# Self-attention in halves of a tile: four heads' scores in a row, in the banks that then hold the other half's transposed probabilities

## The reference, cut to what matters

```
x = cross_attention(x, ctx)                      # (2, 2048, 512), 16 heads, bias, output projection
for layer in range(2):
    h = shift_token(x)                           # the second half of the channels comes from the token before
    q, k, v = split(h @ wqkv, 3)                 # 8 heads of 64
    q = l2norm(q) * q_scale;  k = l2norm(k) * k_scale
    q, k = rotary_xpos(q, k)                     # q*cos*scale + rotate_half(q)*sin*scale, k with 1/scale
    # windows of 256 tokens; a query sees its own window and the one in front, i-256 <= j <= i
    attn = softmax(where(mask, -inf, 8 * q @ k.T))
    x = x + (attn @ v) @ wo
    h = layernorm(shift_token(x)) * lg + lb
    a, g = split(h @ w1 + b1, 2)
    x = x + (a * gelu(g)) @ w2 + b2
```

## Time and profile before

| | us |
|---|---|
| time, median of 3 runs | 3585.88 (3585.81 to 3586.5) |
| the profiled execution | 3587.36 |
| its span | 3585.6 |
| PE busy in the span | 3447.5 (96%) |
| DVE busy | 2271.9 (63%) |
| ACT busy | 1500.6 (42%) |
| POOL busy | 1138.8 (32%) |
| one tile of attention, from transpose to transpose | 22.81 |

### The profile page before, as it was taken

How to read it: one execution, slowest core, us unless ns; L and a number is a source line. 1 busy time by engine, 2 the same in 40 slices (tenths; PEclk the granted TensorE clock), 3 DMA queues, 4 the chain that set the end, 5 groups by cost and what they waited for, 6 DMA issues and landing times. The chain is left out here.

```text
span 3585.6 us, 56360 instructions
## 1 busy us (share of the span) xinstructions
PE 3447.5 (96%) x20560; PEld 2795.2 (78%) x20560; DVE 2271.9 (63%) x4996; ACT 1500.6 (42%) x3978; POOL 1138.8 (32%) x1008
## 2 busy tenths in 40 slices
PE   7999996999999989999999989999999899999999
PEld 5676675888888877888888868888888678888887
DVE  6888875999999984222322259999999642333322
ACT  5666663555555543111111145555555421111111
POOL 3434433555555520000000045555555121101111
PEclk9999998999999999999999989999999999999999
DMA  4112213111121122111111121112111331111111
GB/s 123 42 45 64 71 42 124 57 55 58 61 68 60 57 73 88 44 44 43 42 43 44 64 75 57 57 55 75 57 59 53 97 111 40 46 49 49 40 41 38
DMA packets 186869, 216.26 MB, mean 60 GB/s; under 512 B 27094, under 2 KB 125654, under 8 KB 186595
## 3 DMA queue, kind: packets, MB, share of 16 engines
q1 hardware_dynamic: 186595, 212.65, 18.5%
HBM read 125.79 MB, written 69.00 MB: 54 GB/s over the span
## 5 line engine op out<-in xcount | busy, mean ns | idle before, releaser
L1893 DVE SCALAR_TENSOR_TENSOR u_full<-banks,b_cols,gate 128x512 f32<-128x512 f32 (+1 forms) x176 | 132.1, 751 | 875.4 <-ACT gate L1851 802.4
L46 PE MATMUL banks<-fxT_h,w_h 128*128 128x512 f32 (+1 forms) x1408 | 556.3, 395 | 3.0 <-DVE w_l L1877 2.6
L48 PE MATMUL banks<-fxT_h,w_l 128*128 128x512 f32 (+1 forms) x1408 | 556.1, 395 | 0.0
L47 PE MATMUL banks<-fxT_l,w_h 128*128 128x512 f32 (+1 forms) x1408 | 555.2, 394 | 0.0
L1851 ACT ACTIVATE gate<-banks,b_cols 128x512 f32<-128x512 f32 (+1 forms) x176 | 121.2, 689 | 1007.1 <-PE banks L48 1007.1
L1746 POOL TENSOR_TENSOR sums<-sums,b_rows 128x512 f32<-128x512 f32 x64 | 85.2, 1363 | 877.6 <-DMA sums<-z_rows 877.6
L1146 POOL TENSOR_TENSOR rn<-ssq,neg_half 128x8 f32<-128x8 f32 x128 | 210.8, 1647 | 412.3 <-DVE ssq L1419 405.9
L46 PE MATMUL banks<-wqkv_h,hT_h 128*128 128x512 f32 x768 | 324.9, 423 | 15.0 <-DVE wqkv_l L1406 15.0
L1355 ACT ACTIVATE pT_h<-banks 128x384 fp32r<-128x384 f32 (+2 forms) x512 | 213.9, 470 | 257.5 <-PE banks L1244 256.5
L1460 DVE TENSOR_SCALAR prob<-prob,rc 128x384 f32<-128x384 f32 (+2 forms) x512 | 313.5, 654 | 9.1
L46 PEld LDWEIGHTS banks<-fxT_h,w_h 128*128 128x128 f32 (+1 forms) x1408 | 259.6, 184 | 72.0 <-DVE w_l L1877 4.3
(11 more groups left out here) (190 smaller groups left out, 8183.2 us busy)
## 6 DMA issues: line engine op xcount, KB each, us to landing
y_rows<-sums SPq DMA_DIRECT2D x16, 1024.0 KB
sums<-y_rows SPq DMA_DIRECT2D x64, 256.0 KB, 3.0
z_rows<-sums SPq DMA_DIRECT2D x64, 256.0 KB, 2.0
sums<-z_rows SPq DMA_DIRECT2D x16, 1024.0 KB, 5.8
thirds<-in_w SPq DMA_DIRECT2D x30, 512.0 KB, 4.8
thirds<-in_x SPq DMA_DIRECT2D x8, 1024.0 KB, 6.8
x_rows<-thirds SPq DMA_DIRECT2D x8, 1024.0 KB, 4.3
thirds<-y_rows SPq DMA_DIRECT2D x64, 128.0 KB, 2.8
```

Source lines behind the costliest of these rows:

```text
L46: pe.matmul(out, a_h, b_h, start=start, stop=False)
L47: pe.matmul(out, a_h, b_l, start=False, stop=False)
L48: return pe.matmul(out, a_l, b_h, start=False, stop=stop)
L1893: e.scalar_tensor_tensor(out=u_full[r, m % 2, :], in0=ps[r, 2 * (m % 2), :], scalar=b1[r, place[m], 0:1], in1=gate[r, :], op0=ALU.add, op1 ...
```

## The change

The loop over t has two halves of four heads in place of four rounds of two. PE makes the scores of a whole half in a row: 12 matmuls into four banks, 2 to 5 (`bank_head`). The transposed probabilities of the half in front go into the same four banks, each as soon as the scores that lay there have been masked. `transpose_p` waits for that, and `scores` waits until the transposed probabilities in the banks have been split. In the first half of tile t stand the scores of its heads 4 to 7, v of t + 1, the transpose of t + 2, four transposed heads 0 to 3, q and k of t + 1, the projection of q of t + 2, and the values of heads 0 to 3. In the second stand the scores of heads 0 to 3 of t + 1, the projection of k of t + 2, the transposed heads 4 to 7, the output of t - 1, and the values of heads 4 to 7. `oT` has two buffers. The residual of t - 2 in place of t - 1 is added in tile t. POOL takes root, cosine and sine of q, then those of k. SP issues both copies of keys to the front slots at the same place in its list. The turns in banks 0, 1 and 7 are numbered anew with waits to match.

```
         def bank_qkv(t, a):
-            return turn(7 * t if a == 2 else 7 * t - 2 + a)
+            if (t, a) == (0, 2):
+                return O_BANK
+            return turn(7 * t if a == 2 else 7 * t - 3 + a)
...
+        def bank_head(h):
+            return S_BANK + h % LANES
...
-                    root(0)
-                    times_cos(0)
-                    root(1)
-                    plus_sin(0)
-                    times_cos(1)
-                    plus_sin(1)
+                    for a in range(2):
+                        root(a)
+                        times_cos(a)
+                        plus_sin(a)
...
-                def scores(t, p):
+                def scores(t, half):
...
+                    n = HEADS * t + LANES * half
...
-                    e.wait_ge(s["dv_s"], nth(LH, HEADS * t + 2 * p))
-                    for a, b in ((0, 0), (0, 1), (1, 0)):
-                        for odd in range(2):
...
+                    e.wait_ge(s["dv_s"], nth(LH, n))
+                    e.wait_ge(s["dv_t"], nth(LH, n - LANES))
+                    for p in range(2 * half, 2 * half + 2):
+                        for a, b in ((0, 0), (0, 1), (1, 0)):
+                            for odd in range(2):
...
                 def transpose_p(t, h):
                     n = HEADS * t + h
                     e.wait_ge(s["dv_p"], nth(LH, n + 1))
-                    e.wait_ge(s["dv_t"], nth(LH, n - 1))
+
+                    e.wait_ge(s["dv_s"], nth(LH, min(n + LANES + 1, LH)))
...
+                    if t:
+                        scores(t, 1)
+                    project(t + 1, 2)
+                    transpose_h(t + 2)
+                    if t == 0:
+                        scores(t, 1)
+                    for h in range(LANES):
+                        transpose_p(t, h)
+                    transpose_qk(t + 1)
+                    project(t + 2, 0)
+                    for h in range(LANES):
+                        values(t, h)
+
+                    scores(t + 1, 0)
+                    project(t + 2, 1)
+                    for h in range(LANES, HEADS):
+                        transpose_p(t, h)
+                    output(t - 1)
+                    for h in range(LANES, HEADS):
+                        values(t, h)
...
+                    lo_o(t - 1, 1)
+                    for h in range(LANES, HEADS):
+                        masked(t, h)
+                    residual(t - 2)
+                    lo_v(t + 1)
+                    lo_h(t + 2)
+                    for h in range(LANES):
+                        lo_p(t, h)
+                    lo_qk(t + 1)
+                    divide(t, 2)
+                    norms(t + 2, 0)
+                    divide(t, 3)
...
+                    lo_o(t, 0)
+                    normalise(t + 2, 0)
+                    for h in range(LANES):
+                        masked(t + 1, h)
+                    norms(t + 2, 1)
+                    for h in range(LANES, HEADS):
+                        lo_p(t, h)
+                    normalise(t + 2, 1)
+                    divide(t + 1, 0)
+                    divide(t + 1, 1)
```

More of the change, by code:

```diff
@@ L1099, in body @@
                                 load_piece(e, ahead["s"], w_next, n)
[L1100 to L1104, removed]
+                        if u == 2 and i < NI - 1:
+                            for slot in range(2):
+                                e.wait_ge(s["dv_r"], at(2 * NT, i, 8, 2 * (slot + 2) + 2))
+                                e.wait_ge(s["pe_s"], at(LH, i, 4 * HEADS, HEADS * (slot + 1)))
+                                for part in range(2):
+                                    e.dma_start(kT[part][:, :, slot, :].bitcast(F32), kT[part][:, :, slot + 4, :].bitcast(F32)).then_inc(s["k_copy"], 16)
                         store(i, u - 1)
@@ L1196, in project @@
                     e.wait_ge(s["dv_h"], nth(NT, t + 1))
[L1198 to L1201, removed]
+                    if a == 1:
+                        e.wait_ge(s["dv_r"], nth(2 * NT, 2 * t - 1))
+                    elif a == 2 and t:
+                        e.wait_ge(s["dv_norm"], nth(2 * NT, 2 * t + 1))
                     for k in range(DC):
@@ L1283, in _ @@
                 for t in range(NT):
-                    for p in range(4):
-                        if p < 3:
-                            scores(t, p + 1)
-                        else:
-                            scores(t + 1, 0)
-                        transpose_p(t, 2 * p)
-                        transpose_p(t, 2 * p + 1)
-                        if p == 0:
-                            project(t + 1, 2)
-                        elif p == 1:
-                            transpose_h(t + 2)
-                            output(t - 1)
-                        elif p == 2:
-                            transpose_qk(t + 1)
-                            project(t + 2, 0)
-                        else:
-                            project(t + 2, 1)
-                        values(t, 2 * p)
-                        values(t, 2 * p + 1)
+                    if t:
[17 more added lines that the diff above has]
+                        values(t, h)
                 output(NT - 1)
@@ new lines, in _ @@
+                    lo_o(t - 1, 1)
[4 more added lines that the diff above has]
+                    lo_h(t + 2)
+                    for h in range(LANES):
+                        lo_p(t, h)
[3 more added lines that the diff above has]
+                    divide(t, 3)
+                    if t == NT - 1:
+                        ffn_moments(e, ahead["s"], ahead["t"], l, 0)
@@ new lines, in _ @@
+                    lo_o(t, 0)
+                    normalise(t + 2, 0)
+                    for h in range(LANES):
+                        masked(t + 1, h)
+                    norms(t + 2, 1)
+                    for h in range(LANES, HEADS):
+                        lo_p(t, h)
+                    normalise(t + 2, 1)
+                    divide(t + 1, 0)
+                    divide(t + 1, 1)
+                    if t == NT - 1:
+                        ffn_normalise(e, ahead["s"], ahead["t"], l, 0)
@@ L1537, in _ @@
+                residual(NT - 2)
                 lo_o(NT - 1, 1)
```

128 lines of the change are left out of this document (48 added, 80 removed).

## The result

The changed kernel takes 3670.76 us (median of 4 runs, 3670.17 to 3676.32), the kernel before beside it on the same chip 3586.19 (3585.81 to 3589.21). The ratio is 1.0236, with a 95% interval of 1.0223 to 1.0249: slower by 84.6 us, where I had forecast 56. The time lies 5.8 us above the upper end of the range of my forecast (3665), and 2.8 above that of the 80% range (3668).

A forecast was written before the change was run, and what follows sets the result against it. PE bounds the kernel at 22.81 us a tile; caught divisions would close a 23.56 us cycle: 62 x 0.75 = 47 plus 9 at the starts, 56 more, 3642 us, range 3622 to 3665 (80%: 3577 to 3668).

The forecast's parts named there:

- the catch: DVE's four multiplications behind the `qk` row of k wait for POOL's shared port; next row 4.47 us after the cosine's start.
- the cycle: Chain through DVE, PE, ACT and POOL from one tile to the next: 23.56 us, longer than PE's list of 22.13.
- The term of 47 us: Loss over the 62 steps from tile to tile in both layers, 0.75 us each.
- Rival A: First multiplication behind the `qk` row not caught, so PE's list decides: 22 us less, 3564; chance 0.16.
- PE's list: PE's own work in an attention tile: 22.81 us before, 22.13 after, 0.68 saved by two score groups fewer.
- the starts: Four starts of a sequence, losing between 0 and 4.5 us each, middle 2.3 taken: 9 us together.
- Rival B: First multiplication caught but not the last, as POOL's addition comes later: cycle 22.45, 3582, no change; chance 0.09.
- Rival D: Worse than forecast: clock falls because PE idles, or one more catch of 0.6 on the cycle, 3680; chance 0.05.
- the 0.2 of the working: A caught DVE instruction gets through 0.15 to 0.2 us before the recorded end of POOL's instruction.
- Rival C: PE's four-head score group saves nothing, each pair of heads paying its own way in (0.10 more); no chance given.
- the other edits I cost at nothing: Later residual with store and loads behind it, key copies, second `oT` buffer: zero, POOL's idle time covering the `rot` table.
- The bound of 4.5: Upper limit in us of the loss at each sequence start, where the cycle holds only one half's heads.

The follow-up runs named there:

- tables_early: The changed kernel with the rotation table of a tile loaded one tile earlier, nothing else: 3650.92 us, ratio 1.0175.
- both: The changed kernel with the rotation table one tile earlier and the four divisions in front of the normalise of k: 3561.61 us, ratio 0.9926.
- pool_order: The changed kernel with POOL's old order (root of k between cosine and sine of q), table and divisions as changed: 3593.97 us, ratio 1.0018.
- divide_first: The changed kernel with the four divisions in front of the normalise of k on DVE, the table still late: 3575.42 us, ratio 0.9965.
- all3: The changed kernel with early table, divisions in front of the normalise of k and POOL's old order: 3553.24 us, ratio 0.9907.
- one_behind: The changed kernel with early table and divisions in front, but one of two pairs put back behind the normalise of k: 3570.12 us, ratio 0.995.
- k_short: The changed kernel with early table and POOL's rotation of k on one head of eight, divisions behind the normalise of k: 3556.97 us, ratio 0.9918.

## Why the prediction was wrong in size and right in kind

**Right: the catch and the cycle.** POOL was first by 0.03 us, the four multiplications held DVE for 4.48 us, and the cycle of 23.56 us is what tables_early runs at: 23.55. That sixteen terms meet it to a hundredth is luck, as the working allowed 0.2 either way. Over twelve full steps that kernel is 8.8 us above the one before, 0.73 each, where I had 0.75. The term of 47 us stands. Rival A (not caught) did not occur. Its price came out near: I had 3564 for a kernel with PE's list as the bound, and "both" takes 3561.61. Part of that is luck: in the profile the full steps give 28 us back (48 of 0.59), the starts take 12, and another 9 come back outside the steps of the layers, which A's sum did not have. Rival B would have needed POOL's addition to come late; the fourth multiplication was caught for 1.51. Rival D's clock stayed at 1.00 in the full tiles; it fell behind one long wait in each layer, and at the starts of the layers it was lower than before (both below). In the Trainium skill, SBUF — State Buffer, section SBUF: two separate sides, the loser is blocked for the whole of the other's instruction; the trace agrees up to the end: the first multiplication went through from 1118.69 (1117.63 + 1.48 - 0.42), POOL's cosine ends in the record at 1118.89, so 0.20 earlier. It is the 0.2 of the working, once more.

**Nearly right: PE's list.** I had 0.68 us saved a tile; it is 0.59. The scores come in groups of 12 (PE's timeline of the changed kernel):

```profile
1118.66 0.22 PE L48 MATMUL banks<-pT_h,v_l 128*64 128x128 f32 x1
1118.82 0.45 PE L1246 MATMUL banks<-kT_h,qT_h 64*128 64x384 f32 x2
...
1119.46 0.34 PE L1246 MATMUL banks<-kT_h,qT_h 64*128 64x384 f32 x2
...
1120.09 0.50 PE L46 MATMUL banks<-wqkv_h,hT_h 128*128 128x512 f32 x1
1120.42 0.39 PE L47 MATMUL banks<-wqkv_l,hT_h 128*128 128x512 f32 x1
```

From the first scores to the projection it is 1.27 us, 0.09 goes before, and the projection's first step is 0.33 where a usual one is 0.23, so 0.10 behind: 1.46 for a group, where I had 0.87 + 0.53 = 1.40, and a list of 22.81 - 4 x 0.87 + 2 x 1.46 = 22.25. The missing number was the projection behind scores, 0.10 and not the 0.05 of a transpose. Two groups make 0.12 by these prices, where the lists differ by 0.09 (0.68 - 0.59), and it is in no sum that decides here, since PE waits anyway. Rival C is refuted: the second pair of heads costs 0.54 (1.27 - 0.73), three steps as forecast, and no way in of its own.

**Wrong: "the other edits I cost at nothing".** I let POOL's idle time cover the table of `rot`. POOL's idle time is not what is short; the time between the residual, behind which SP issues the table, and POOL's product is. The residual of t - 2 comes half a tile later, and behind it SP issues the store, the loads of rows, and then the table. In the tile shown above, SP's store and the table:

```profile
1125.58 0.32 SPq L1084 DMA_DIRECT2D z_rows<-sums  x1
...
1127.87 1.27 SPq L1077 DMA_DIRECT2D rot<-in_rot  x1
```

From the store's issue to POOL's product (1131.37) it is 5.8 us. The term that I had put at nothing costs 19.8 us (3670.76 - 3650.92). Two thirds of it stand behind the start of the second sequence, where four steps are 12.8 and 12.6 us above the kernel before in the two layers, and 6.0 in both with the table early (13.4 less together). Nearly all of that is one tile in each layer. SP's queue in the first of them, with the length of each issue:

```profile
1026.11 0.32 SPq L1084 DMA_DIRECT2D z_rows<-sums  x1
1026.47 0.29 SPq L1087 DMA_DIRECT2D z_late<-sums  x1
1026.80 1.46 SPq L1097 DMA_DIRECT2D sums<-y_rows  x1
1028.31 1.82 SPq L971 DMA_DIRECT2D thirds<-y_rows  x1
1030.17 0.43 SPq L972 DMA_DIRECT2D thirds<-y_late  x1
1030.65 0.43 SPq L1077 DMA_DIRECT2D rot<-in_rot  x1
```

then POOL, whose root of q had its clamped sum at 1031.90 and starts at 1037.54, 5.6 us after it:

```profile
1036.74 0.72 POOL L1148 TENSOR_TENSOR rot<-rot,qk_scale 128x256 f32<-128x256 f32 x1 [12.40 <-DMA rot<-in_rot]
1037.54 1.65 POOL L1156 TENSOR_TENSOR rn<-ssq,neg_half 128x8 f32<-128x8 f32 x1
```

then PE:

```profile
1040.54 2.09 PE L1258 MATMUL banks<-ident,prob 128*128 128x128 f32 x8 [4.53 <-DVE neg_m L1463]
```

and its clock, in windows of 5 us (columns as in the earlier trace rows):

```profile
1036.00:1041.00 5.00, 0.47 (x3) 0.30 (x3) 1.78 (x6) 0.60 (x1) 3.38 (x3) 0.81 0.00 1
1041.00:1046.00 5.00, 5.00 (x16) 3.85 (x16) 3.24 (x11) 3.92 (x12) 4.53 (x5) 0.51 0.01 3
1046.00:1051.00 5.00, 5.00 (x47) 4.23 (x46) 4.93 (x8) 0.75 (x2) 4.19 (x4) 1.00 0.00 0
```

Two issues of SP last 1.46 and 1.82 us in place of 0.45, the table leaves at 1030.65 and is used at 1036.74; the root of q, the `qk` row and the masks come after it one by one, PE stands still for 4.53 us, and behind that the granted clock is 0.51, the 1.2 GHz level, for some 5 us: there 128x512 matmuls start 0.43 us apart (1043.28, 1043.70) in place of 0.23. This tile takes 29.9 us from transposes to transposes, its like in the second layer 29.4. The rest of the 20 us is a steady tile that wanders between 23.5 and 24.3 instead of standing at 23.56. In the wandering POOL's root of q starts right behind the late product (1132.18 behind 1131.37, above). How the 0.7 us by which it is held turn into the single values I have not followed.

**Wrong in size: the starts.** I took 2.3 us for each of four starts. With the table out of the way (tables_early) the four steps around the start of the second sequence are 6.0 us above the kernel before in each layer, or 3.0 each beyond the 0.75 a step, as forecast within its bounds. But the first five steps of the layers are 12.7 and 13.3 above, so 9.0 and 9.6 beyond it. The bound of 4.5 took the same cycle as in a full tile, only with fewer heads. What bounds a start is another thing. The first five steps of the first layer take 106.5 us before and 118.8 changed, 12.3 more. With POOL's old order alone they are 4.4 more (110.9, pool_order), with the divisions in front alone 4.9 more (111.4, divide_first), with both and the early table 1.4 more (107.9, all3). POOL's new order alone, in the kernel before, costs 3.8. So the halves by themselves cost 1.4 there, the divisions behind 3.0 and POOL's order 3.5 when each comes alone, and the two together 10.9. Nor does the clock stay up there, as it does in a full tile. Windows of the kernel before and of the changed one at the start of the first layer (columns as in the earlier trace rows):

```profile
600.00:640.00 40.00, 31.86 (x188) 25.26 (x188) 23.47 (x77) 16.77 (x51) 25.19 (x25) 0.91 0.00 1
```

```profile
600.00:640.00 40.00, 28.55 (x136) 22.29 (x136) 20.87 (x62) 11.72 (x37) 22.03 (x21) 0.74 0.00 0
```

PE idles more, and the granted clock is 0.74 in the mean in place of 0.91. How much of the 12.3 us is waiting and how much the lower level is not separated by any run. What I had not counted either is the time outside the steps of the layers: in the profiles it is 6.2 us shorter than before in the changed kernel and 3.2 in tables_early, and I have no run that says why.

**The sum, by what ran.** Cycle 47; table 19 (within the steps of the layers); starts 25 (9.0 + 9.6 + 3.0 + 3.0) in place of 9; outside the steps less 6: 85. The spans of the two profiles differ by 83.2, the medians by 84.6. Two steps of the prediction failed, then. The table, put at nothing, measured 19.8: without it the changed kernel is at 3651, inside the range. The starts, put at 9 and at most 18, measured 25: with 9 for them the time would have been some 3655, inside as well. It took both to leave the range. Still open: how the start of a layer splits between waiting and clock; what shortens the rest of the span; and why two issues of SP took over a microsecond.

## What to carry to other kernels

Behind a row for which another engine waits that shares a port with yours, put the work that cannot be caught: the order of two calls was worth 95 us here, and the four caught instructions became free when they stood in front, where POOL had nothing to do. Judge it by the length of the cycle that the held work closes, not by the catches: half of them stayed in one_behind, three other ones came up in all3, and neither cost the full tiles anything. And when a step that gates a queue moves, follow each DMA behind it to its user with its landing time, and look at the starts of a sequence by themselves, where the bound is another one.

## What the hardware showed that I had not expected

- Two engines that are released by the same row: 0.03 us (1117.60 and 1117.63) decide who holds the port, the same way in changed, one_behind (1127.89 and 1127.92) and k_short (1116.01 and 1116.03).
- Of DVE's caught multiplications one gets in between two of POOL's instructions, each time: 1.48, 0.89, 0.70, 1.51 under cosine, sine, sine, addition. The catch is as long as POOL's instruction lets it be, down to 0.51 us in all under a cosine of 0.32.
- The same DMA of 128 KB took 3.4 us from issue to landing at 1127.87 and 6.0 at 1030.65, both times behind the same store and loads of rows. The issues themselves lasted between 0.3 and 1.8 us in these two places, and one 2.87 us in the second layer (2570.72).
- Behind PE's stop of 4.53 us the granted clock was 0.51 for some 5 us; in the full tiles, where 1.32 us of waiting lie in short pieces, it stayed at 1.00.
- A busy PE may be a waiting PE: 23.34 us of busy time for a list of 22.22.
